# Stores of turned parts ahead of the next tile's work, and two of the second batch's four tiles prepared beside the attention

## What is computed

```python
x = x + _layernorm(_L0_attn_ref(_layernorm(x), ...))   # 16 heads of 16, rope, causal
x = x + _layernorm(_L0_ffn_ref(_layernorm(x), ...))    # 8 experts, 2 chosen
x = x + _layernorm(_L1_attn_ref(_layernorm(x), ...))   # below
x = x + _layernorm(_L1_ffn_ref(_layernorm(x), ...))    # 64 experts, 4 chosen, 2 shared
```

```python
q = (x @ wq.T).reshape(B, T, NH, 2, HH)...             # k likewise, v = x @ wv.T
q1, q2 = _rotary(_rms_norm(q[..., 0, :])), _rotary(_rms_norm(q[..., 1, :]))
k1, k2 = _rotary(_rms_norm(k[..., 0, :])), _rotary(_rms_norm(k[..., 1, :]))
y = _causal_attn(q1, k1, v, scale) - lam * _causal_attn(q2, k2, v, scale)
y = y @ wo.T * (1.0 - LAMBDA_INIT)
```

## Time and profile before

| | us |
|---|---|
| median of 3 runs | 561.92 |
| the three runs | 562.53, 556.06, 561.92 |
| the profiled execution | 556.62 |
| its span in the trace | 554.8 |

### The profile page before, as it was taken

One profiled execution on the slowest core, in us unless ns is written; L12 is line 12 of the kernel. 1 busy time (PEld: TensorE's weight loads), 2 busy tenths in 40 slices (PEclk: granted clock), 3 DMA queues, 4 the chain that ended last, 5 costly groups with the idle time before them and its releaser, 6 DMA issues.

```text
span 554.8 us, 9043 instructions
## 1 busy us (share of the span) xinstructions
PE 432.3 (78%) x2742; PEld 285.2 (51%) x2742; DVE 321.6 (58%) x1049; ACT 257.9 (46%) x543; POOL 182.4 (33%) x297
## 2 busy tenths in 40 slices
PE   1787676998878668476789695988986999999970
PEld 1443333344444345363334542534645999999860
DVE  5657677655343375925622714535598666666758
ACT  2322224344456414446552575333166777777404
POOL 6011001222123401312230332110006777778770
PEclk9998875555798779969889898689796999999995
DMA  7790020000000000000000030119943666656632
GB/s 235 251 349 27 1 57 2 0 2 1 1 0 2 1 0 19 1 1 1 1 1 0 1 116 0 40 33 390 374 151 82 191 192 190 192 188 184 185 103 95
DMA packets 37754, 50.72 MB, mean 91 GB/s; under 512 B 3664, under 2 KB 29264, under 8 KB 37712
## 3 DMA queue, kind: packets, MB, share of 16 engines
q1 hardware_dynamic: 33104, 37.60, 20.0%
q0 software_dynamic: 4608, 12.59, 8.6%
HBM read 31.30 MB, written 18.87 MB: 90 GB/s over the span
## 4 chain that ended last, share of the span: by engine, by line
PE 64%; DVE 20%; ACT 7%; issue 6%; DMA 1%; POOL 1%; SPq 0%; DVEq 0%; POOLq 0%; ACTq 0%
PE PSUM L785 11%; PE PSUM L1105 11%; PE PSUM L729 6%; PE PSUM L1092 5%; PE PSUM L799 4%; PE PSUM L757 3%; PE PSUM L735 3%; PE PSUM L1083 3%; PE PSUM L923 3%; PE PSUM L950 2%; DVE st L1407 2%; PE PSUM L942 2%; PE PSUM L722 2%; PE PSUM L858 2%; ACT PR L1173 2%
## 5 line engine op out<-in xcount | busy, mean ns | idle before, releaser
L1173 ACT ACTIVATE PR<-PSUM 128x1024 f32<-128x1024 f32 (+1 forms) x96 | 81.6, 880 | 61.9 <-PE PSUM L799 61.6
L652 POOL TENSOR_SCALAR_AFFINE_SELECT PR<-PR 128x256 f32<-128x256 f32 x128 | 51.2, 416 | 161.9 <-ACT PR L1173 160.8
L1502 DVE CUSTOM_DVE_ANT_0 XN<-PSUM,XN 128x128 f32<-128x128 f32 (+3 forms) x128 | 56.2, 488 | 37.5 <-PE PSUM L757 37.3
L1105 PEld LDWEIGHTS PSUM<-QP,XT 128*128 128x128 f32 x512 | 68.6, 195 | 3.4 <-ACT QP L1362 0.2
L1105 PE MATMUL PSUM<-QP,XT 128*128 128x128 f32 x512 | 69.0, 279 | 0.0
L785 PE MATMUL PSUM<-PR,VA 128*32 128x256 f32 (+3 forms) x512 | 60.8, 571 | 8.8 <-DVE XT L1552 8.8
L799 PE MATMUL PSUM<-QT,KTr 32*128 32x384 f32 (+7 forms) x256 | 45.3, 431 | 13.4 <-ACT PR L1173 10.8
L757 PE MATMUL PSUM<-KTr,QT 32*128 32x128 f32 (+3 forms) x128 | 39.3, 536 | 12.7 <-DVE mx L1502 12.3
L519 POOL TENSOR_TENSOR QP<-QK,QP 128x128 f32<-128x128 f32 (+1 forms) x16 | 9.8, 610 | 118.6 <-ACT KP L507 67.3
L799 PEld LDWEIGHTS PSUM<-QT,KTr 32*128 32x128 f32 (+1 forms) x256 | 24.2, 223 | 45.7 <-issue 26.1
L685 POOL DMA_INDIRECT QP<-tokens,tok_of x24 | 23.8, 990 | 58.6 <-DVE tok_of L1823 51.6
(11 more groups left out here) (260 smaller groups left out, 790.2 us busy)
## 6 DMA issues: line engine op xcount, KB each, us to landing
expert_outputs<-PR SPq DMA_DIRECT2D x1, 8192.0 KB, 26.5
arena<-in_wgu SPq DMA_DIRECT2D x4, 2048.0 KB, 15.8
expert_outputs<-QP SPq DMA_DIRECT2D x64, 128.0 KB
arena<-in_wd SPq DMA_DIRECT2D x2, 2048.0 KB, 18.1
wq_sb<-in_wqkv SPq DMA_DIRECT2D x2, 768.0 KB, 5.4
X<-in_x SPq DMA_DIRECT2D x2, 512.0 KB, 4.4
QP<-in_wsgu SPq DMA_DIRECT2D x1, 1024.0 KB, 5.5
tokens<-XN SPq DMA_DIRECT2D x2, 512.0 KB, 6.7
```

The costliest lines, as they stand in the source:

```text
L652: ins = pool.affine_select(diag, diag, [[0, 2], [1, P]], ALU.is_ge, 0.0, base=0, channel_multiplier=-1)
L1105: mm = pe.matmul(bank(2 + 2 * part + r % 2)[:, 0:P], WB[:, r, w0:w0 + P], XGT[:, r, kt * P:(kt + 1) * P], start=(kt == 0), stop=(kt == KT ...
L1173: did(sc.activation(PR[:, n % PSLOTS, 2 * half:2 * half + 2, 0:WIDTH[chunk]], PSUM[:, 2 * half:2 * half + 2, 0:WIDTH[chunk]], ACT.Exp, sca ...
L1502: did(dv.tensor_tensor_reduce(MSK[m % 2][:, 0:nk], o[:, 0:nk], MASKQ[:, S - nk:S], op0=ALU.add, op1=ALU.max, scale=1.0, scalar=NEG, accum_ ...
```

## The change

Two parts. First, on ACT and on DVE the store piece of a tile stands ahead of the more and project pieces (DVE) and of the project piece (ACT) of the same step, and in BETWEEN batch 1's LN1 and ADD1 come later, ADD1 behind the last of the preparation. Second, tiles 0 and 1 of batch 1 are apart, tile 1 is projected at PREP + 2 (attention step 20), and tiles 2 and 3 at PREP + 9 and PREP + 10 (attention steps 27 and 28). PE's waits for banks are adapted to that.

```diff
-TILE_AT = ((0, 1, 2, 3), (0, 6, 7, 8))
+TILE_AT = ((0, 1, 2, 3), (0, 2, 9, 10))
 def apart(b, i):
-    return b == 1 and i < 1
+    return b == 1 and i < 2
...
-           (0, PREP + 2), (1, LN1), (0, PREP + 3), (0, PREP + 4), (1, ADD1), (0, PREP + 5), (0, PREP + 6))
+           (0, PREP + 2), (0, PREP + 3), (1, LN1), (0, PREP + 4), (0, PREP + 5), (0, PREP + 6), (1, ADD1))
...
-                        if apart(b, i - 1):
+                        if apart(b, i - 1) and not apart(b, i):
                             pe.wait_ge(s_tevk, 2 * c)
                             pe.wait_ge(s_tev, 2 * NT + 2 * c)
...
                     if apart(b, i):
-                        pe.wait_ge(s_qkve1, c + 1)
-                        pe.wait_ge(s_ve, c + 1)
-                    elif i == b:
+                        pe.wait_ge(s_qkve1, b * TB + 2)
+                        pe.wait_ge(s_ve, b * TB + 2)
+                    elif i == 2 * b:
                         pe.wait_ge(s_p, (b + 2) * STEPS)
...
-                            had = 2 * c + half if apart(b, i) and half else 2 * (c - 1) + half + 1
-                            if apart(b, i) and not half or i == b and not apart(b, i):
+                            had = 2 * c + half if apart(b, i) else 2 * (c - 1) + half + 1
+                            if i == 0 and not half or i == 2 * b and not apart(b, i):
                                 had = 0
```

24 lines of the change are left out of this document (12 added, 12 removed).

## The result

The changed kernel takes 564.76 us in the median of 20 executions (558.97 to 568.99), the kernel before 559.01 in the median of 20 (553.62 to 562.53). The ratio is 1.0086, with a 95% interval of 1.0054 to 1.0118. So it is a little slower, within 2%, where I had forecast 1.6 us less. The profiled execution took 558.97, one of the shortest; its span is 557.2 against 554.8, so it shows only 2.4 us of the loss.

The account below looks back on a forecast made before the run. PE bounds the kernel, losing time to idle waits and its lower clock. A (batch 0's preparation) -2.4 plus B +0.8 gives -1.6 us: 560.3 from the median 561.92 (555.0 from the profiled 556.62), range 552.5 to 564.0.

Parts of the forecast that it names:

- First scores 5.1 us earlier: Batch 0's preparation: earlier stores shorten PE's waits before the turns, so the first attention scores come 5.1 us earlier.
- ADD1 gives 2.7 of it back through ACT's queue: Start of attention: ADD1 now follows the preparation; NORM2's root waits for it, holding later exponentials; 2.7 of 5.1 us returned.
- So step 1 and everything behind comes only 2.4 us earlier: From attention step 1 on: everything, including the turn of normalised tokens, moves 2.4 us earlier.
- Quad 3's first product 3.1 later: Batch 1, step 21: tile 1's projection, square and copy delay the exponential, sums and evacuation, so this product comes 3.1 us later.
- Its length of 3.25: Quad 3's first product keeps its earlier price of 3.25 us; at full clock it would be 1.3 less.
- 2.3 less in front of tile 2's turn: Batch 1: tile 1's turn and the 4.15 us KTr wait go, a 3.8 us s_pad wait comes; 2.3 us less.
- The last two turns stay at 5.04: Batch 1, tiles 2 and 3: turns after a 3.8 us gap still take 5.04 us, partly at the lower clock.
- B: Batch 1's preparation: 3.1 + 0.0 - 2.3 = 0.8 us more, bounds -2.1 and about +3.5.
- Nothing else changes: Later stages: same instructions, merely moved 1.6 us; any other length behind the last attention's first scores would show the prediction wrong.
- rival 3: Batch 1: tile 1's square and copy delay step 21, leaving PE at 1.2 GHz up to the projections; +1.1 us, 15 in 100.
- Rivals 1 and 2: 1: all waits vanish, ADD1 hides, about -9 us, 6 in 100; 2: clock stays up in B, -4.0, 17 in 100.
- Rival 4: Batch 0's preparation gains only 0.9 us because tile 3 turns at the lower clock; with B no change, 17 in 100.

Follow-up runs that it names:

- e1: Kernel before with only the stores ahead and later LN1 and ADD1, batch 1's tiles at old places; mean 561.6 us against 559.6 before, ratio 0.993.
- e6: Changed kernel with batch 1's tile 1 projected one step later, at PREP + 3; mean 600.9 us against 593.2 for the kernel before, ratio 1.014.
- e11: Changed kernel with batch 1's tile 1 at PREP + 4, tiles 2 and 3 at PREP + 10 and 11; mean 559.0 us against 559.7 before.
- e12: e11 plus unread transposes in four of PE's waits (24, 16, 20, 20); mean 548.2 us against 559.7 for the kernel before, ratio 0.984.
- e4: The changed kernel once more, unaltered; mean 562.5 us against 559.6 for the kernel before, ratio 1.001.
- e9: The changed kernel again, unaltered, in another group; mean 562.9 us against 559.7 for the kernel before, ratio 1.005.
- e14: Kernel of e1 plus unread transposes in four of PE's waits; mean 580.9 us against 588.1 for the kernel before without them, ratio 0.987.
- e5: Kernel of e1 plus 20 unread transposes before the turn at step 2; mean 590.9 us against 593.2 for the kernel before, ratio 0.988.
- e8: Changed kernel plus 20 unread transposes before the turn at step 2, 16 before tile 2's turn; mean 591.7 us against 593.2 before, ratio 0.996.
- e10: Same kernel as e8, in the group of e9; mean 561.9 us against 559.7 for the kernel before, ratio 1.005.

## Why the prediction was wrong, by its own steps

- **First scores 5.1 us earlier**: 5.15 (31.08 to 25.93). Right, with its path: tile 1 turned right behind tile 3's projection, at 223.00, which is 223.75 on the scale of before. That all turns run at 1.94 was not right: tile 2's ran at the lower clock, hidden by the wait for tile 3's `s_pad`.
- **ADD1 gives 2.7 of it back through ACT's queue**: right. The turn at step 2 comes 6.38 behind the first scores instead of 3.58, so 2.35 of the gain was left there; 2.4 was forecast.
- **"So step 1 and everything behind comes only 2.4 us earlier"**: this step failed. I carried the 2.4 along as a shift and never asked what the wait of 4.27 us does to the clock behind it, though I had read just that in the earlier trace rows for another wait. The clock was low at the turn before the change, too (0.50 from 241.8 to 248.7). In the changed kernel it stayed low longer, 0.9 us up to the first product, and fell again at the gates, 1.1 more net. Up to the up-projection all but 0.3 was lost again (25.93 + 6.38 + 7.58 + 6.93 + 3.96 = 50.8 against 51.1), at PEclk 0.50 and 0.56; in e1's trace another 2.5 go in the next stretch.
- **Quad 3's first product 3.1 later**: 3.2 (13.48 against 10.24), released by DVE's evacuation. Right, with its path: 2.78 by PE's projection in front of step 21's scores, the rest by ACT's square and copy. DVE's queue, which I had not looked at, costs nothing here but 2.35 us in e6.
- **Its length of 3.25**: 3.43. The rule of the Trainium skill (TensorE: Matmul & The Clock Gate, "What's actually happening"), that the clock falls after an idle window, would have made it 1.3 less. Here too the clock was low with a wait of only 1.64 in front, so the trace speaks against it once more. In e11 and e12 it took 1.86 and 1.85 behind tile 1's projection.
- **2.3 less in front of tile 2's turn**: the wait for KTr went, and POOL's took its place with 3.27 instead of 3.8. The term was right to half a us, and POOL's second subtraction took 0.72 us, for which I had given 2.8 less.
- **The last two turns stay at 5.04**: mis-sized, 6.50 at PEclk 0.56. I had argued that a wait of 3.8 does what one of 4.15 did. It was the largest miss in B: forecast +0.8, measured +2.1 (10.24 + 3.25 + 26.88 = 40.4 before, 42.5 after).
- **"Nothing else changes"**: 1.3 us more behind it in the profiled execution, in stages with the same instructions (1.4 and 1.3 in e4 and e9). This was one of my own signs of being wrong; the other, first scores outside 314.5 to 321, did not come (320.97).
- **The rivals**: rival 3 had the right side and the wrong place. The projections ran at full clock (1.98), and the low clock was at the start of the attention and in the last turns. Rivals 1 and 2 did not come. Rival 4 had the right thought, A given back by the clock, at the wrong instructions. None of them had the size.
- **The range**: it ended at 564.0, and the median is 564.76. I took the spread of the executions as noise around a level that the change leaves alone. It goes with the clock; part of it lies ahead of the change, and with the change the low clock came more often. The median moved by 5.75 us, the mean of the same executions by 5.0 and that of the 44 against the 63 by 3.7; what the longest executions of the changed kernel are made of is not traced.

What stays open is why the clock falls in one execution of the same kernel and not in the next, and at the gates in one kernel and not in the other behind waits of the same length. No run moves the wait at step 2 in time and leaves its length. e12 and e14 show that work in the waits takes the loss away in these stretches; e5, e8 and e10, with one and two fills, point the same way but are too weak by themselves.

## What to carry to other kernels

A gain that leaves an engine idle behind it is not a shift: for TensorE the price of a wait is the wait and the clock behind it, so look at the windows for both kernels before carrying a saved microsecond along. Where executions of one kernel differ, set time against the mean granted clock: if two kernels agree at equal clock, the net difference is how often the clock is low (their parts may still cancel, as here), and one profiled execution does not show it. Look in the trace, too, whether two executions already differ ahead of the change. Before moving a piece beside other work, look on every engine for what it now stands in front of.
